# Building a 0/1 edge matrix from groups of 5 targets with one block of 128 edges each, instead of groups of 25 with four

## What is computed

```python
def _sage(x, src, dst, W_l, b_l, W_r):
    msg_sum = jax.ops.segment_sum(x[src], dst, num_segments=N_NODES)
    cnt = jax.ops.segment_sum(jnp.ones((src.shape[0],), x.dtype), dst, num_segments=N_NODES)
    aggr = msg_sum / jnp.maximum(cnt, 1.0)[:, None]
    return aggr @ W_l.T + b_l + x @ W_r.T
h_fwd = _sage(x, src, dst, ...)
h_bwd = _sage(x, dst, src, ...)
```

## Time and profile before

| | |
|---|---|
| median of 3 runs | 1440.79 us (1439.73 to 1441.76) |
| span of the profiled execution | 1624.1 us |
| what lies around the span | not listed; no separate time of that execution |
| VectorE busy over the span | 774.9 us (48%) |
| GpSimd busy | 641.0 us (39%) |
| TensorE matmuls busy | 1260.9 us (78%) |
| first gather of edge records issued | 21.43 us |
| last one issued | 155.20 us |
| first and last window matmul | 65.3 and 328.2 us |

### The profile page before, as it was taken

One profiled execution on the slowest core, in us unless ns is written; L12 is line 12 of the kernel. 1 busy time (PEld: TensorE's weight loads), 2 busy tenths in 40 slices (PEclk: granted clock), 3 DMA queues, 4 the chain that ended last, 5 costly groups with the idle time before them and its releaser, 6 DMA issues. The chain is left out here.

```text
span 1624.1 us, 22613 instructions
## 1 busy us (share of the span) xinstructions
PE 1260.9 (78%) x7483; PEld 943.8 (58%) x7483; DVE 774.9 (48%) x2286; ACT 456.2 (28%) x916; POOL 641.0 (39%) x723
## 2 busy tenths in 40 slices
PE   3521899998777458781768999999899887993997
PEld 2310666795446346560556777777687664553886
DVE  4420899922766653336434444454335533224332
ACT  2200666612312222220222333333233223231110
POOL 4576005800040336661066566566656600001442
PEclk9755899999988569996889999999999998996999
DMA  4000000003100612225545555555555505549551
GB/s 92 3 3 3 2 2 2 2 2 85 19 0 1 227 44 81 77 79 129 160 145 168 151 176 165 162 170 176 160 165 173 154 10 180 154 105 235 163 180 63
DMA packets 99733, 165.22 MB, mean 102 GB/s; under 512 B 18181, under 2 KB 61812, under 8 KB 99234
## 3 DMA queue, kind: packets, MB, share of 16 engines
q1 hardware_dynamic: 71649, 90.65, 19.9%
q0 software_dynamic: 27968, 73.08, 15.3%
HBM read 138.06 MB, written 27.63 MB: 102 GB/s over the span
## 5 line engine op out<-in xcount | busy, mean ns | idle before, releaser
L2272 POOL DMA_INDIRECT em_gathered<-edge_table,el_which x313 | 301.9, 965 | 191.0 <-DVE em_hidden L2362 112.6
L2284 PE MATMUL em_projected<-em_w,em_attr 128*128 128x256 f32 x1252 | 296.0, 390 | 26.5 <-DVE em_hidden L2362 11.7
L2284 PEld LDWEIGHTS em_projected<-em_w,em_attr 128*128 128x128 f32 x1252 | 242.5, 196 | 72.9 <-issue 39.2
L2362 DVE TENSOR_TENSOR em_hidden<-em_projected,em_gathered 128x512 f32<-128x512 f32 (+1 forms) x157 | 107.1, 684 | 196.7 <-PE em_projected L2284 107.3
L2384 ACT ACTIVATE em_hidden<-em_hidden 128x512 f32<-128x512 f32 (+1 forms) x157 | 98.4, 627 | 257.2 <-DVE em_hidden L2362 203.0
L567 PE MATMUL nm_banks<-nm_hot_key,nm_hot_a 128*125 128x500 bf16 x400 | 124.5, 408 | 44.3 <-issue 36.4
L451 DVE TENSOR_SCALAR nm_hot_key<-nm_key_order,ek_keys 128x500 bf16<-128x500 int16 x400 | 137.8, 360 | 0.0
L450 DVE TENSOR_SCALAR nm_hot_a<-nm_order,ek_places 128x125 bf16<-128x125 int16 x320 | 84.2, 263 | 80.7 <-remote 64.3
L252 POOL DMA_INDIRECT nm_adj<-in_edge_records,ek_record_at x100 | 94.9, 949 | 43.5 <-issue 29.9
L567 PEld LDWEIGHTS nm_banks<-nm_hot_key,nm_hot_a 128*125 128x125 bf16 x400 | 50.0, 141 | 92.7 <-issue 42.3
L435 POOL TENSOR_SCALAR nm_hot_a<-nm_order,ek_places 128x125 bf16<-128x125 int16 x80 | 58.2, 743 | 112.4 <-DVEq L444 104.9
(11 more groups left out here) (485 smaller groups left out, 2277.4 us busy)
## 6 DMA issues: line engine op xcount, KB each, us to landing
em_attr<-in_edge_attr_sets SPq DMA_DIRECT2D x156, 256.0 KB
oe_table<-state SPq DMA_DIRECT2D x20, 448.0 KB
oe_wd<-in_ffn_Wd SPq DMA_DIRECT2D x8, 1024.0 KB
em_gathered<-edge_table,el_which POOLq DMA_INDIRECT x313
mx_w<-in_ffn_w SPq DMA_DIRECT2D x16, 256.0 KB
oe_table<-state SPq DMA_DIRECT2D x1, 2248.8 KB
state<-in_x SPq DMA_DIRECT2D x5, 448.0 KB
state<-in_x SPq DMA_DIRECT2D x1, 2240.0 KB
```

The lines of the kernel that those rows point to most:

```text
L2272: nc.gpsimd.indirect_dma_start(out=gathered[:, n % GATHERED, :], out_offset=None, in_=table, in_offset=bass.IndirectOffsetOnAxis(ap=lanes. ...
L2284: last = nc.tensor.matmul(projected[:, k % BANKS, n % 2, :], attr[:, k % ATTR_RING, (n % 2 * KB + f) * 128:(n % 2 * KB + f + 1) * 128], w1 ...
L2362: nc.vector.tensor_tensor(pair_slots(k), projected[:, k % BANKS, 0:width, :], gathered[:, at:at + width, :], ALU.add).then_inc(pre_ready, 1)
```

## The change

- 500 windows of 5 targets, five of them a strip of 25. A window's edges are one block of 128, from an edge number rounded down to a multiple of 4. `hot_key` has 100 columns (20 tiles by 5 targets), and each product stands alone in 100 columns of the PSUM bank. `keep_window` keeps a strip, in the order tile, window, target.
- A record is now the 128 sources and 132 targets from such an edge number on. 125 windows lie on the partitions, so four gathers fetch all of them, and four more before them the rows of 125 edges: 8 for 101.
- Places and keys are found for all windows at once (`vector_keys`, before the second part of the normalisation), with a window per partition; TensorE turns them in 8 transposes (`ek.tensor`, now ahead of the second part's `turn_rows`), and VectorE copies them from PSUM (`vector_keep`).
- The ring holds four strips. VectorE signals TensorE once a strip, not once a block, and TensorE frees a strip, not a block. Four strips are built between the last `keep_low` calls, where one window was.
- GpSimd builds `hot_a` of one window in even strips and of two in odd ones, 150 in all, from the first strip on. TensorE waits for them before a strip.
- The test for `general_sums` is now whether a window of 5 reaches past its 128 edges. The largest of these inputs, counted from its rounded start, has 106.

```diff
-WINDOW = 25
+STRIP = 25
+STRIPS = NODES // STRIP
+WINDOW = 5
 WINDOWS = NODES // WINDOW
+PER_STRIP = STRIP // WINDOW
...
     def pool(self, pool):
         pool.wait_ge(self.block_found, 1)
-        nc.gpsimd.indirect_dma_start(out=self.edge_row, out_offset=None, in_=self.A["dst_rows"], ...
+        for g in range(self.GROUPS):
+            nc.gpsimd.indirect_dma_start(out=self.edge_row[:, g], out_offset=None, in_=self.A["dst_rows"], ...
         pool.wait_ge(self.record_found, 1)
+        for g in range(self.GROUPS):
+            nc.gpsimd.indirect_dma_start(out=self.records[:, g], out_offset=None, in_=self.A["edge_records"], ...
...
+        for g in range(self.GROUPS):
+            last = nc.vector.tensor_scalar(self.less[:, g], self.firsts, self.limit[:, g:g + 1], None, ALU.is_lt)
...
+    def vector_keys(self, dve):
+        src, dst, next_dst = self.records[:, :, 0:128], self.records[:, :, 128:256], self.records[:, :, 256:257]
+        dve.wait_ge(self.got, self.GROUPS * 16)
+        chain.tick(nc.vector.tensor_scalar(self.coarse, src, 4195, None, ALU.mult))
+        chain.wait(dve)
+        nc.vector.tensor_tensor(self.past[:].unsqueeze(2), self.limit[:].unsqueeze(2), next_dst, ALU.subtract)
+        chain.tick(nc.vector.tensor_scalar(self.coarse, self.coarse, 19, None, ALU.arith_shift_right))
+        chain.wait(dve)
+        nc.vector.scalar_tensor_tensor(self.place, self.coarse, float(-P), src, ALU.mult, ALU.add)
+        chain.tick(nc.vector.scalar_tensor_tensor(self.key, dst, float(TILES), self.coarse, ALU.mult, ALU.add))
+        chain.wait(dve)
+        nc.vector.tensor_tensor(self.key, self.key, self.base[:].unsqueeze(2).broadcast_to([P, self.GROUPS, 128]),
+                                ALU.subtract).then_inc(self.keys_found, 1)
...
+    def vector_keep(self, dve, ready):
+        dve.wait_ge(self.keys_turned, 1)
+        nc.vector.tensor_copy(self.places[:], self.places_turned)
+        nc.vector.tensor_copy(self.keys[:], self.keys_turned_bank).then_inc(ready, 1)
...
     def tensor(self, pe):
+        pe.wait_ge(self.keys_found, 1)
+        for g in range(self.GROUPS):
+            nc.tensor.transpose(self.places_turned[:, g * P:(g + 1) * P], self.place[:, g], self.ident[:P, :P])
+            last = nc.tensor.transpose(self.keys_turned_bank[:, g * P:(g + 1) * P], self.key[:, g], self.ident[:P, :P])
+        last.then_inc(self.keys_turned, 1)
...
-    RING, BATCHES = 2 * SPAN, 4
+    BATCHES, RING = 4, 4
-    BY_POOL, SHARED = (1, 3), 6 * ek.AT_ONCE
+    BY_POOL = ((1,), (1, 3))
+    pool_hots = lambda w_: w_ // 2 * 3 + w_ % 2
...
+                pool.wait_ge(keys_ready, 1)
+                for w_ in range(STRIPS):
+                    if w_ >= RING:
+                        pool.wait_ge(hot_used, w_ - RING + 1)
+                    for s in BY_POOL[w_ % 2]:
+                        n = w_ * PER_STRIP + s
+                        nc.gpsimd.tensor_scalar(hot_a[:, w_ % RING, s, :], order[:], ek.places[:, n:n + 1], None,
                                                 ALU.is_equal).then_inc(pool_hot_ready, 1)
...
+                def build(w_):
+                    if w_ >= RING:
+                        dve.wait_ge(hot_used, w_ - RING + 1)
+                    for s in range(PER_STRIP):
+                        n = w_ * PER_STRIP + s
+                        if s not in BY_POOL[w_ % 2]:
+                            nc.vector.tensor_scalar(hot_a[:, w_ % RING, s, :], order[:], ek.places[:, n:n + 1], None, ALU.is_equal)
+                        last = nc.vector.tensor_scalar(hot_key[:, w_ % RING, s, :], key_order[:].rearrange("p b d -> p (b d)"),
+                                                       ek.keys[:, n:n + 1], None, ALU.is_equal)
+                    last.then_inc(hot_ready, 1)
...
                 for t in range(low, TILES):
                     keep_low(t)
                     step = t - low
+                    if step % 2 and step // 2 < RING:
+                        build(step // 2)
...
+                    pe.wait_ge(hot_ready, w_ + 1)
+                    pe.wait_ge(pool_hot_ready, pool_hots(w_ + 1))
+                    for s in range(PER_STRIP):
+                        last = nc.tensor.matmul(acc[:, w_ % 2, s * KEYS:(s + 1) * KEYS], hot_a[:, w_ % RING, s, :], hot_key[:, w_ % RING, s, :],
+                                                start=True, stop=True)
+                    last.then_inc(hot_used, 1)
...
+                    nc.scalar.activation(adj_T[:, t % 2, :, j * STRIP:(j + 1) * STRIP].rearrange("p b (s d) -> p b s d", s=PER_STRIP),
+                                         acc[:, w_ % 2, 0:PER_STRIP * KEYS].rearrange("p (s b d) -> p b s d", s=PER_STRIP, b=TILES),
+                                         ACT.Copy).then_inc(window_kept, 1)
```

More of the change, by code:

```diff
@@ L202 @@
 class EdgeKeys:
-    AT_ONCE, STEPS = 10, 5
-    GROUPS = WINDOWS // AT_ONCE
+    GROUPS = WINDOWS // P
     def __init__(self, p, c, A, adj, wide, scope):
         nc = self.nc = p.nc
-        self.A, self.ident, self.ones, self.wide = A, c.ident, c.ones, wide
+        self.A, self.ident, self.wide = A, c.ident, wide
+        G = self.GROUPS
         sb = lambda name, shape, dtype=F32: p.sb("ek_" + name, shape, dtype, scope)
         sem = lambda name, recycled=True: p.sem("ek_" + name, recycled)
[L213 to L235, removed]
@@ new lines, in __init__, with spare @@
+        self.most = sb("most", [1, 1])
+        late = adj[:, TILES - 5:, :].rearrange("p t n -> p (t n)")
+        taken = 0
+        def spare(dtype, *shape):
+            nonlocal taken
+            size = math.prod(shape)
+            part = late.bitcast(dtype)[:P, taken:taken + size]
+            taken += size
+            return part.rearrange("p (g n) -> p g n", g=shape[0]) if len(shape) > 1 else part
+        self.firsts, self.less = spare(I32, EDGE_TILES), spare(F32, G, EDGE_TILES)
+        self.ordered, self.falls = spare(I32, EDGE_TILES + 1), spare(F32, EDGE_TILES)
@@ L530, in _ @@
                 dve.wait_ge(made, 1)
+                ek.vector_keep(dve, keys_ready)
+                dve.wait_ge(keys_ready, 1)
                 for t in range(low, TILES):
@@ L533, in _ @@
                     step = t - low
-                    if step < ek.STEPS:
-                        ek.find_keys(dve, 0, step)
-                    elif step < ek.STEPS + SPAN // 2:
-                        build(0, 2 * (step - ek.STEPS), 2 * (step - ek.STEPS) + 2)
-                for w_ in range(1, WINDOWS):
+                    if step % 2 and step // 2 < RING:
+                        build(step // 2)
+                for w_ in range(RING, STRIPS):
                     build(w_)
@@ L624, in _ @@
                         project(t)
-                ek.tensor_order(pe)
+                ek.tensor_order(pe, keys_ready)
                 pe.wait_ge(copied, TILES)
-                for w_ in range(WINDOWS):
+                for w_ in range(STRIPS):
                     build(w_)
```

176 lines of the change are left out of this document (62 added, 114 removed).

## The result

| | before | after |
|---|---|---|
| median of the runs, us | 1440.26 (1435.18 to 1441.76) | 1414.39 (1410.68 to 1415.98) |
| ratio | | 0.9825, interval 0.9809 to 0.9841 |
| span of the profiled execution, us | 1624.1 | 1414.0 |

The change makes the kernel faster by 26 us; the forecast was 1411.0, a gain of 30. The spans in the table fall by 210 us, the runs by 26. That gap turned out to be the most instructive part of the case. Ratios leave out one execution of experiment 2, of 1550.34 us at a granted clock of 0.806, where the other eight took 1428.26 to 1435.40.

A forecast was written before the change was run, and what follows sets the result against it. VectorE was taken to bound the windows. Windows of 189 us become 153, plus 6 us moved ahead, 159: a gain of 30 us on 1440.8 gives 1411, range 1392 to 1432.

The forecast's parts named there:

- VectorE bounds before and after: In the windows VectorE sets the pace: 1.795 or 1.68 us a window before, 1.59 us a strip after.
- Step (1): VectorE's one-hots in the windows: a 100-column key one-hot costs 0.159 us, five make 0.80 us a strip.
- the case of cheap small one-hots: Rival: key one-hots in the windows cost only 0.08 us, 37 us more gained, 1374 us; 14 in 100.
- Step (2): GpSimd's 150 hot_a beside VectorE in the windows: each costs VectorE 0.11 us, 0.17 us a strip.
- Step (3): The windows of the kernel before: 175 us, plus 16 us for 80 gathers at 0.2 each, together 191.
- Step (4): Work moved ahead of the windows (starts, keys, copies, builds) adds 6 us.
- that cover: VectorE measuring x and sizing the weights while the four dst_rows gathers run, so that they cost nothing instead of 4 us.
- A cost of the recorded execution, absent from the runs: The held stretches at and before the windows, 99 us, belong to the profiled execution, 183 us longer than the runs' median.
- real in the runs: Rival: the held stretches occur in the runs, wholly or half; 45 to 99 us more gained, middle 1350; 10 in 100.
- I am wrong if the runs fall as much as the span: Sign against the forecast, which expected the span to fall far more than the runs, by 120 us or so.
- both slower cases: Rivals in the windows: TensorE's clock falls, 1461 us, 9 in 100; GpSimd and VectorE exclude each other, 1497, 3 in 100.

The follow-up runs named there:

- experiment 2: The kernel before with 20 gathers of edge records instead of 100, later groups reusing the first two groups' records: ratio 0.9972 to the kernel before.
- experiment 7: The changed kernel with VectorE building only one of five key one-hots a strip past the first four strips: 1456.87 us, 40.3 less than the changed kernel there.
- experiment 1: The kernel before, unchanged, profiled once more: 1438.68 us, span 1436.6, against a median of 1435.63 for the kernel before on that chip.
- experiment 3: The changed kernel with all 500 hot_a on VectorE and none on GpSimd: 1423.18 us, ratio 0.9921 to the kernel before.
- 8: The changed kernel with GpSimd building two of five place one-hots in every strip, 200 instead of 150: 1492.98 us against 1497.17.

## Why the prediction was right, and where it was not

The time fell within 3.4 us of the forecast. The mechanism held; that the number came so close is in part luck, as three terms of the sum were off and nearly cancelled.

- **VectorE bounds before and after: right.** For after experiment 7 shows it, since taking away VectorE's work alone gives 40 us. For before the trace of experiment 1 speaks: VectorE is busy 65.88 of 66 us and TensorE waits for its key one-hots 177 times; no run took work away there.
- **Step (1), 100 columns at 0.159 us: right**, 0.155 measured. The line through two sizes held, and the case of cheap small one-hots is out. (Its bound of 0.08 us is 0.09 in the earlier trace rows.)
- **Step (2), 0.11 us for a GpSimd one-hot: mis-sized**, it is 0.07 (experiment 3, borne out by 8). With the smaller steps, 0.78 + 0.58 + 0.04 + 0.10 = 1.50 us a strip, where 1.49 was measured and 1.59 forecast: 96 x 0.10 = 10 us too much. In the sum only 7 of them show: at the first window matmul the fourth strip and two `keep_low` were still to come, some 3 us that the 96 strips leave out.
- **Step (3), windows before at 191 us: mis-sized.** They take 180.0. The 60 and 40 windows at 175 were right (175.5 with 20 gathers); the 80 gathers cost 4.5 us and not 16. The 0.39 us over two gathers was read where the rows were dense, in a profile of the other kind of chip, and didn't stand for the other 78.
- **Step (4), 6 us ahead of the windows: mis-sized**, it is 8.5. Of the four dst_rows gathers the text said "nothing; without that cover 4 us". The cover was not there: VectorE waits 4.04 us. The gathers were indeed out by 15.4 us, as forecast, but that was taken for their end, and the 8.2 us from issue to landing, which the trace of before had, was left out. With this wait the terms come to 10 us and 8.5 was measured, so the others were 1.5 too high together; no run splits that.
- The sum: 189 forecast for 180 in before, 153 for 146.2 in after, 6 for 8.5. The errors of the windows, 9 and 7, nearly cancel in the difference; by the traces the gain is 33.8 - 8.5 = 25.3, not 30.
- **"A cost of the recorded execution, absent from the runs": right for the runs, wrong in what it was taken for.** The median of 1440.79 showed that the runs had no such stretch, and the sum made against them held. But the stretch was no accident of a recording. On two of the four chips the kernel before takes some 187 us longer in every run, and on the one of them where it was tried taking away 80 gathers alone is worth 89 us. Nor do all 183 us sit in the held stretches: against experiment 1, 187.5 us shorter in span, the windows start 16 us later and take 83 more, and 89 lie behind them. The rival "real in the runs" had 10 in 100 and a middle gain of 91 us in all; on such a chip the gain is 125, outside the forecast.
- **"I am wrong if the runs fall as much as the span": they do.** On one chip the time of an execution and its span are always some 2 us apart, so both fall alike. The fall of 210 us in the spans compares two kinds of chip: some 125 of it are the change on the slower kind, 83 the chip.
- TensorE's clock was 1.00 from 80 to 200 us, and GpSimd and VectorE don't exclude each other in these single-input instructions (0.07 us each, where the case needed 0.32): both slower cases are out.

## What to carry to other kernels

When the profiled span and the timed runs differ by more than a per cent, ask first whether they are of the same chip, and time the kernel on more than one before you call a stretch a fault of the recording: a change can be worth 26 us on one and 125 on another. A DMA moved ahead is costed along its own chain, from what starts it to its landing, 8 us behind its issue here, and not by the free time of the engine that will read it. Before one-hots are shared with GpSimd, see which form VectorE uses: single-input ones leave GpSimd nearly undisturbed, two-input ones slow it by half.

## What was not expected of the hardware

- Indirect gathers issued one after another hold up the other three engines on one kind of chip: 1.11 us a gather of 1.25 us spacing on the one chip where they were taken away, against 0.06 on one of the other kind. Most instructions keep their durations and start late; the profile puts the idle time down to "remote" and "issue".
- GpSimd's comparison of 125 columns takes 0.67 us beside single-input VectorE instructions and 1.02 beside two-input ones, whether these fill most of VectorE's time or under half of it.
- ScalarE's copy with the new order of its 500 elements costs nothing: 605 ns a piece, 606 before.
- The indirect gathers at the start, beside the load of x with the DMA engines full (share 1.00 from 10 to 22 us), land 8.0 to 8.9 us after their issue; the record gathers behind it take 3.9. That the load is the cause is not tested.
